# Masked attention: the three mask steps of the next batch in slots 0, 1 and 1 in place of 0, 2 and 4

## The reference, cut to what matters

```python
q, k, v = heads(Q @ W_q.T + b_q), heads(K @ W_k.T + b_k), heads(V @ W_v.T + b_v)   # 16 heads of 8
q, k, v = nan_clamp(q), nan_clamp(k), nan_clamp(v)
bias = clip(nan_clamp(attn_bias), -10000, 10000)          # [1, 16, 56, 1500]
logits = einsum('bhqd,bhkd->bhqk', q, k) * scale + bias
logits = where(mask == 0, -10000.0, logits)               # mask: [32, 1, 56, 1500], int32
out = einsum('bhqk,bhkd->bhqd', softmax(logits), v)
out = merge_heads(out) @ W_o.T + b_o
```

## Time and profile before

| | |
|---|---|
| runs | 6157.67, 6165.86, 6163.29 us |
| profiled execution | 6152.64 us, span 6150.5 us |
| PE, DVE, ACT, POOL busy in the span | 86%, 73%, 52%, 30% |
| batch from 758.80 to 801.34 us | 42.54 us |
| PE, DVE, ACT, POOL busy in it | 37.84, 37.69, 28.87, 30.31 us |

### The profile page before, as it was taken

The page is one execution under the profiler, slowest core; times in us unless marked ns, Lnnn a source line. Parts: engine busy times, 40 slices in busy tenths (PEclk is TensorE's granted clock), DMA queues, the critical chain, the costliest instruction groups (busy, mean ns, idle before and its releaser), DMA issues. The chain is left out here.

```text
span 6150.5 us, 133121 instructions
## 1 busy us (share of the span) xinstructions
PE 5287.2 (86%) x51447; PEld 3802.1 (62%) x51447; DVE 4466.4 (73%) x9168; ACT 3193.4 (52%) x6024; POOL 1844.2 (30%) x1456
## 2 busy tenths in 40 slices
PE   1888989888669999989839999999999749999997
PEld 1777777777258888877824444444444427888885
DVE  6898898986357777763457777777777547777776
ACT  0666666666246666652224444444444216666663
POOL 4777676772022222211001111111111022222220
PEclk6999999999689999999969999999999869999998
DMA  4555565553167777743010000000000048888981
GB/s 107 124 131 126 127 129 125 131 125 80 37 122 140 140 140 139 140 81 115 24 31 21 16 15 15 15 15 15 15 15 10 7 91 151 163 161 161 161 155 30
DMA packets 368544, 545.53 MB, mean 89 GB/s; under 512 B 115780, under 2 KB 248006, under 8 KB 367606
## 3 DMA queue, kind: packets, MB, share of 16 engines
q1 hardware_dynamic: 365894, 533.81, 42.9%
q0 software_dynamic: 2048, 3.67, 0.2%
HBM read 413.45 MB, written 123.90 MB: 87 GB/s over the span
## 5 line engine op out<-in xcount | busy, mean ns | idle before, releaser
L653 DVE CUSTOM_DVE_ANT_0 attn_logits<-attn_scores,attn_shift 112x750 f32<-112x750 f32 x1024 | 944.9, 932 | 440.3 <-PE attn_scores L457 440.0
L569 ACT ACTIVATE attn_probs_t<-attn_pt 125x448 f32<-125x448 f32 x1536 | 829.6, 541 | 581.7 <-PE attn_pt L472 561.1
L472 PEld LDWEIGHTS attn_pt<-ident,attn_logits 112*125 112x125 f32 x6144 | 851.6, 189 | 179.7 <-issue 92.8
L472 PE MATMUL attn_pt<-ident,attn_logits 112*125 112x112 f32 x6144 | 920.7, 273 | 26.4 <-ACT attn_logits L560 24.8
L2246 PE MATMUL attn2k_pk<-attn_wk,attn2k_cn_t 128*125 128x512 f32 x1536 | 738.8, 603 | 53.0 <-ACT attn2k_cn_t L2317 36.7
L2257 PE MATMUL attn2k_pg<-attn2k_kn,attn2k_cn 125*128 125x512 f32 x1536 | 725.0, 594 | 6.0 <-ACT attn2k_gram L2325 3.9
L2412 DVE TENSOR_REDUCE attn2k_ss<-attn2k_sq 125x16 f32<-125x1024 f32 x384 | 466.9, 1216 | 257.7 <-ACT attn2k_sq L2354 257.6
L386 POOL CAST attn_k_parts<-xn_t 128x500 bf16<-128x500 f32 x192 | 199.3, 1038 | 1422.6 <-DVE xn_t L623 1422.6
L2354 ACT ACTIVATE attn2k_sq<-attn2k_pk 125x1024 f32<-125x1024 f32 x384 | 391.5, 1019 | 324.8 <-PE attn2k_pk L2246 324.6
L1165 ACT ACTIVATE attn_probs_t<-attn_pt 125x448 f32<-125x448 f32 x768 | 413.8, 539 | 275.0 <-PE attn_pt L1053 273.0
L2246 PEld LDWEIGHTS attn2k_pk<-attn_wk,attn2k_cn_t 128*125 128x125 f32 x1536 | 273.1, 187 | 416.7 <-issue 320.8
(11 more groups left out here) (363 smaller groups left out, 10434.9 us busy)
## 6 DMA issues: line engine op xcount, KB each, us to landing
attn_k_packed<-k_scratch SPq DMA_DIRECT2D x384, 375.0 KB, 6.4
attn_k_packed<-k_scratch SPq DMA_DIRECT2D x384, 187.5 KB, 4.4
k_scratch<-attn_k_parts SPq DMA_DIRECT2D x64, 1125.0 KB, 7.6
attn_ctx_t<-in_ctx_t SPq DMA_DIRECT2D x64, 750.0 KB, 7.4
k_scratch<-attn_k_parts SPq DMA_DIRECT2D x96, 375.0 KB, 3.7
attn_ctx_t<-in_ctx_t SPq DMA_DIRECT2D x96, 250.0 KB, 4.1
attn2k_ctx<-in_ctx SPq DMA_DIRECT2D x32, 750.0 KB
attn_mask_in<-in_mask SPq DMA_DIRECT2D x192, 109.4 KB
```

The source lines that it names most:

```text
L472: last = pe.transpose(pt[(3 * at + t) % 2][0:KC, (c % 4) * PAIR:(c % 4 + 1) * PAIR], logits[:, at % 3, c * KC:(c + 1) * KC], g.ident[0:PAI ...
L569: act.activation(probs_t[0:KC, p // 4, 4 * t:4 * t + 4, (p % 4) * PAIR:(p % 4 + 1) * PAIR], pt[(3 * at + t) % 2][0:KC, 0:QUAD].rearrange(" ...
L653: dve.tensor_tensor_reduce(out=logits[:, at % 3, cols].rearrange("p (b k) -> p b k", b=2), in0=scores[h][0:PAIR, :, 0:QTR], in1=shift[:, n ...
```

## The change

DVE makes the second step after the first `shifted` of slot 1 and the third at the end of slot 1; before, they stood in slots 2 and 4. On SP's queue the third mask load moves up, between the key loads of part 2 and part 3, and the load of the transposed mask goes behind the key loads.

```diff
@@ block.sync
                     if n + 1 < B:
                         load_keys(n + 1, 0, (0, 1))
                         load_mask(n + 1, 1)
-                        load_keys(n + 1, 0, (2, 3))
+                        load_keys(n + 1, 0, (2,))
+                        load_mask(n + 1, 2)
+                        load_keys(n + 1, 0, (3, 4, 5))
                     load_mask_t(n)
-                    if n + 1 < B:
-                        load_mask(n + 1, 2)
-                        load_keys(n + 1, 0, (4, 5))
@@ block.vector
-                        if p in (0, 2, 4) and n + 1 < B:
-                            mark(n + 1, p // 2)
+                        if p < 2 and n + 1 < B:
+                            mark(n + 1, p)
                         if p == 5:
                             mark_t(n)
                         shifted(n, p, 1)
...
                         negate(n, p)
+                        if p == 1 and n + 1 < B:
+                            mark(n + 1, 2)
```

## The result

The changed kernel takes 6217.1 us (median of 4 runs, 6211.74 to 6221.98) against 6164.57 us of the kernel before on the same chip: 1.0084, 95% interval 1.0067 to 1.0102, or +52.5 us. The forecast of 6180 had the sign; the time is 37 us above it and 13 above the range's end of 6204.

What follows compares the result with a forecast made beforehand. The prediction took a chain of PE, DVE through slots 2 to 5, then PE again to set the period. +0.5 us over 29 batches (14.5), with the ends some 17 us, gave 6180 us as median; range 6138 to 6204.

Steps and rivals of the forecast that it cites:

- The second step: Slot 1: held behind GpSimd's tensor_tensor, ending 0.28 us past it at 765.54, inside DVE's idle time until 767.46.
- The third step: End of slot 1: waits for its load (3.4 us), then held by GpSimd to 770.45; slot 2 starts 2.9 us late.
- PE's 3.04 us before slot 5: PE's wait for DVE before the second half of slot 5, forecast to become smaller.
- The sum for SP's queue: Key loads and `load_mask_t` go later, behind the third mask load; all of it put at nothing.
- The forecast's own case: Third step held twice, GpSimd's chain late; landing 3.27 to 4.45 us after issue; 6171 to 6191 us, chance 0.48.
- wrong if the third steps are short: Sign against the forecast: third steps of 0.4 us (load early or much later), where 1.3 to 1.5 us was forecast.
- Where it is lost again: Split keys 2.0 us late make GpSimd's second values late; DVE takes them 0.85 us late, leaving +0.5 us per batch.
- gain of 1.5 from the two steps removed: Mask steps leaving slots 2 and 4 take 0.73 + 0.76 = 1.5 us per batch off DVE's pace-setting stretch.
- The queue is quiet: Reason for taking 3.4 us for the third mask load: the next key load stands behind it.
- The load lands before 768.84: Rival: landing under 3.27 us after issue, GpSimd's values in time; -0.5 us per batch, 6148 us, chance 0.22.
- The load is hidden: Rival: third step ends by 768.3, slots 2 to 5 keep most of 1.5 us; near 6125 us, chance 0.10.
- A crowded queue: Rival: the load takes 5.51 us, slot 2 late by 4.0; +1.6 us per batch, 6209 us, chance 0.12.

Runs made afterwards that it cites:

- f2: Against f1: one mask load, all three mask steps in slot 0, the first 500 keys' mask standing for all 1500; ratio 1.0001 to before, batch 43.18 us.
- f1: Changed kernel without the third mask load, so the third step reads the second's data and can't wait; ratio 1.0014 to before, batch 43.15 us.
- light guard: GpSimd's guard of the values cut to one of three operations: before (h0) 41.21, f1 (h1) 40.71, changed kernel (h2) 42.43 us a batch.
- e1: Changed kernel, the key loads and transposed-mask load behind the third mask load held until the third step has run; ratio 1.0084 to before, batch 44.50 us.
- e4: Changed kernel with the third mask step in slot 2 instead of the end of slot 1, loads unchanged; ratio 0.9988 to before, batch 42.56 us.
- h1: f1 with GpSimd's guard of the values cut to one of three operations; ratio 0.9874 to before, batch 40.71 us.
- e3: Kernel before with the second mask step alone moved to slot 1, the third left in slot 4; ratio 1.0031 to before, batch 43.31 us.

## Why the prediction was wrong, point by point

**Right.** The second step: forecast to be held by the tensor_tensor to its end plus 0.28 us, in time that DVE has; 1.45 us, and f2 shows that it costs nothing. The third step: a wait for the load (28 times). In the batch of 826.63, set against the batch from 801.34 before, it is also held, with slot 2 late by 2.81 us where 2.9 was forecast, and the split keys 1.90 us late where 2.0 was. The cast back to 0.42 us. PE's 3.04 us before slot 5 down (2.08 us in the batch of 826.63). DVE's wait for PE before slot 2 gone. The sum for SP's queue on the keys and `mark_t`: nothing waited for them.

**The forecast's own case was rare.** The landing of 3.27 to 4.45 us that it needs came in 6 of 28 batches; 13 were earlier and 9 later. The third step took 1.26 to 1.45 us in 3 batches and 0.42 to 0.94 in the others. By the sign that the prediction set itself ("wrong if the third steps are short") it was wrong there, and that the mean lateness of the head, 1.53 us, is not far from its 2.0 is chance: early and late landings balance.

**The step that failed** is "Where it is lost again": the +0.5 us per batch that was to be left of the 2.0 us of lateness. It measured +2.03. The step took two durations as fixed that are not, a term of nothing each. First GpSimd's chain of 20.0 us from the split keys to the second values: in the late batch it took 20.99, since operations that now met DVE's steps at other places grew (line 939 from 0.60 to 1.06 us, line 951 from 1.18 to 1.61, line 940 from 2.10 to 2.32), more than others shrank. DVE took the values 1.65 us late, not 0.85; the margin itself was sized rightly (the values were ready 2.89 us late, 1.24 of it absorbed). Second DVE's own steps behind the values: `finite` went from 0.41 to 0.81 us and line 1363 from 0.39 to 0.87, together 0.88. So 1.65 + 0.88 = 2.53 us, and the 0.3 us that PE was to absorb at the end were not absorbed: the batch is 44.88 - 42.32 = +2.56 against the batch from 801.34 to 843.66 before. The step on `out_t` in slot 5 grew most, from 0.50 to 1.98 us (to 858.14, 0.37 us past the end of `q_blocks`), but it is not in this sum: DVE waits 0.42 us for the values behind it.

Split by experiments: the wait, 1.66 us per batch (after - f1; 1.72 with the light guard), passed on with slope 1; and +0.37 us in place of the gain of 1.5 from the two steps removed. I had counted that gain on DVE's side, and it did arrive in part (the second `shifted` of slot 4 came 0.27 us early in the late batch, 1.44 us in that of 1233.21, forecast 0.5 to 0.9). f1 shows where it went: DVE takes the values only 0.55 us earlier than before, since the longer chain makes them ready 0.91 us later and it has to wait, and the stretch behind them is 0.92 us longer. The margin that was to absorb the lateness is thus gone before the load is even waited for, to the longer chain and to DVE's coming early.

**Smaller misses.** "The queue is quiet" was wrong: 0.9 MB is issued behind the load within some 2 us, and e1 shows that this makes the landings over 4.4 us. One landing of 3.4 us was taken for all; they run from 2.5 to 6.15, with 13 of 28 below the 3.27 that decided between forecast and gain. The estimate of 2.65 us is near the quick half (2.5 to 3.1) and has nothing of the slow one. The Trainium skill, "DMA: Bandwidth & Descriptors", section "Anatomy of one DMA — SWDGE (gpsimd) path", gives its 2.0 us and 436 GB/s for a DMA that GpSimd issues; this load is issued by SP.

**The rivals.** *The load lands before 768.84* happened in 13 of 28 batches and was refuted in its price: they gained nothing (that of 1233.21 is +1.0 us, not -0.5), since even 0.7 us of lateness goes into the batch. *The load is hidden* is e4: slots 0, 1, 2, and it is worth 0.22 us per batch, not 1.5. *A crowded queue*, 6209, is the nearest in size for the wrong reason: its 5.51 us was reached in three batches.

**Open.** Why GpSimd's operations and DVE's steps hold one another as they do at each place, so that the next order could be priced; whether, in h1, DVE's longer steps are the whole of the 1.0 us that is missing; whether instruction fetches cause the slow landings.

## What to carry to other kernels

A margin that is read from two timestamps holds only as long as nobody between them is moved: where two engines hold one another, the length of a chain is itself a result, and lateness at its head should be priced whole unless the margin is shown to survive the change itself (here the two moved steps alone used it up). Work removed from an engine that is then early for its neighbour's long operation is not gained; look for what it will run into. And a single buffer read twice in one slot puts a whole load's time, with its spread of 2.5 to 6 us, on the path; one slot in between (e4) took it off.

## What the hardware showed that I had not expected

GpSimd's operations stretch as well as DVE's: the same 1456 instructions took 39 us more over the span. A mask step, `finite` or cast on DVE that started inside a GpSimd tensor_tensor ended 0.28 us past it each time, in before, after and e3, but beside line 940's tensor_scalar it took 0.41, 0.65 or 0.81 us depending on where in it it started (1.15, 1.50 and 0.56 us in; the 0.65 us too ended 0.28 us past it); the whole-instruction lock that the Trainium skill states ("SBUF — State Buffer", "Who interferes with whom") is seen for the first kind here and not for the second. The same mask load of 218.8 KB took, in e1, 2.5 to 3.0 us in 17 batches and 3.5 to 4.4 in 14, with no other difference found in the traces than when a packet of 16 KB of instruction fetch started; only above that did other loads matter.
